# Attention and expert kernel: logits from 64-row f32 products of queries and keys, in place of split f32r products through a combined weight

## The reference, cut to what matters

```python
Q = (X @ Wq + bq).reshape(b, t, h, dq).transpose(0, 2, 1, 3)
K = (X @ Wk).reshape(b, t, h, dq).transpose(0, 2, 1, 3)
V = (X @ Wv).reshape(b, t, h, dq).transpose(0, 2, 1, 3)
R = (X @ Wr + br).reshape(b, t, h, nb).transpose(0, 2, 1, 3)
extra = jnp.einsum('bhtn,ntp->bhtp', R, D_ntT)
logits = jnp.einsum('bhtd,bhpd->bhtp', Q, K) / math.sqrt(dq) + bias + extra
W = jax.nn.softmax(logits, axis=-1)
A = jnp.einsum('bhtp,bhpd->bhtd', W, V)
return A.transpose(0, 2, 1, 3).reshape(b, t, h * dq) @ Wproj + bproj
```

## Time and profile before

| | |
|---|---|
| median of 3 runs | 1675.25 us (1672.22 to 1677.1) |
| profiled execution | 1675.05 us, its span 1673.3 us |
| PE busy | 1510.8 us, 90% |
| VectorE busy | 1066.7 us, 64% |
| ScalarE busy | 988.9 us, 59% |
| GpSimd busy | 804.1 us, 48% |
| mean granted TensorE clock | 0.958 |
| chain that ended last, by engine | PE 72%, DVE 9%, issue 8%, ACT 4% |

### The profile page before, as it was taken

The page is one execution under the profiler, slowest core; times in us unless marked ns, Lnnn a source line. Parts: engine busy times, 40 slices in busy tenths (PEclk is TensorE's granted clock), DMA queues, the critical chain, the costliest instruction groups (busy, mean ns, idle before and its releaser), DMA issues.

```text
span 1673.3 us, 42585 instructions
## 1 busy us (share of the span) xinstructions
PE 1510.8 (90%) x10864; PEld 1276.9 (76%) x10864; DVE 1066.7 (64%) x3749; ACT 988.9 (59%) x2999; POOL 804.1 (48%) x1515
## 2 busy tenths in 40 slices
PE   2555999999999999989999997998989898989997
PEld 2224887878878887878999996787878787877885
DVE  5585777777767777762211112787868786877775
ACT  2223776766766676755554443676757675766664
POOL 0322766666666666650000001665656565656654
PEclk8686999999999999999999998999999999999999
DMA  9774555655555555655666664565555555656552
GB/s 285 271 274 120 163 168 145 177 166 165 155 160 168 152 159 145 180 154 160 201 202 205 206 202 136 155 174 135 167 143 161 150 149 143 166 142 180 145 158 70
DMA packets 375709, 282.62 MB, mean 169 GB/s; under 512 B 16626, under 2 KB 349988, under 8 KB 375588
## 3 DMA queue, kind: packets, MB, share of 16 engines
q1 hardware_dynamic: 367396, 264.64, 53.9%
q0 software_dynamic: 8192, 16.79, 3.5%
HBM read 168.05 MB, written 113.26 MB: 168 GB/s over the span
## 4 chain that ended last, share of the span: by engine, by line
PE 72%; DVE 9%; issue 8%; ACT 4%; SPq 3%; DMA 2%; DVEq 1%; POOL 1%; ACTq 0%; POOLq 0%
PE ps L1336 11%; PE ps L1334 11%; PE ps L1335 11%; PE ps L1475 10%; PE ps L1433 10%; PE ps L1370 8%; PE ps L1487 6%; PE ps L1404 3%; ACT prob L826 2%; DVE logit L1137 2%; DVE gst L1088 1%; DVE probT L1111 1%; DVE acc L1176 1%; SPq L453 1%; PE ps L1352 1%
## 5 line engine op out<-in xcount | busy, mean ns | idle before, releaser
L826 ACT ACTIVATE prob<-logit,low 128x128 f32<-128x128 f32 (+1 forms) x1024 | 454.2, 446 | 149.4 <-DVE low L1137 123.3
L1111 DVE COPY probT<-ps 128x384 f32<-128x384 f32 x512 | 284.5, 556 | 204.5 <-PE ps L1433 192.6
L687 POOL TENSOR_SCALAR prob<-prob,inv 128x128 f32<-128x128 f32 x512 | 188.6, 368 | 346.3 <-DVE inv L1121 336.7
L1137 DVE CUSTOM_DVE_ANT_0 logit<-ps,extra 128x128 f32<-128x128 f32 (+1 forms) x1024 | 303.3, 353 | 0.7 <-PE ps L1336 0.4
L1433 PE MATMUL ps<-ident,prob 128*128 128x128 f32 x1536 | 264.0, 281 | 12.1 <-DVE probT L1111 7.3
L1475 PE MATMUL ps<-probT,val 128*64 128x256 f32 (+1 forms) x2048 | 203.1, 342 | 44.1 <-DVE probT L1111 42.7
L689 POOL TENSOR_SCALAR prob<-prob,inv 128x256 f32<-128x256 f32 x512 | 241.4, 472 | 0.0
L1475 PEld LDWEIGHTS ps<-probT,val 128*64 128x64 f32 x2048 | 131.8, 141 | 130.7 <-issue 82.6
L1433 PEld LDWEIGHTS ps<-ident,prob 128*128 128x128 f32 x1536 | 175.0, 142 | 48.2 <-issue 40.7
L1334 PE MATMUL ps<-key_hi,xq_hi 128*128 128x256 f32 (+1 forms) x512 | 194.9, 381 | 0.0
L826 ACT ACTIVATION_READ_ACCUMULATOR prob<-logit,low 128x1 f32 x1024 | 192.9, 188 | 0.0
(11 more groups left out here) (188 smaller groups left out, 3088.2 us busy)
## 6 DMA issues: line engine op xcount, KB each, us to landing
skew<-gst SPq DMA_DIRECT2D x256, 256.0 KB
extra<-skew SPq DMA_DIRECT2D x128, 512.0 KB, 3.9
extra<-skew SPq DMA_DIRECT2D x128, 256.0 KB, 3.6
w1b<-w_d SPq DMA_DIRECT2D x39, 514.0 KB, 3.5
w2b<-w_d SPq DMA_DIRECT2D x39, 320.0 KB, 3.3
x_place<-zero SPq DMA_DIRECT2D x39, 256.0 KB, 2.7
placed<-x_place SPq DMA_DIRECT2D x39, 256.0 KB, 3.7
y_place<-yrow SPq DMA_DIRECT2D x39, 256.0 KB, 2.2
```

What stands on the lines that cost most here:

```text
L687: nc.gpsimd.tensor_scalar(prob[:, h, 0:P], prob[:, h, 0:P], inv[:, h, 0:1], 1.0, ALU.mult, ALU.mult).then_inc(norm_made, 1)
L826: ins = nc.scalar.activation(prob[:, h % PB, a:b], logit[:, h % LB, a:b], ACT.Exp, scale=-1.0, bias=low[:, h % LB, t:t + 1], accum_out=tot ...
L1111: nc.vector.tensor_copy(probT[:, h % 4, :], ps[:, PT_BANK, 0:3 * P]).then_inc(pT_made, 1)
L1137: ins = nc.vector.tensor_tensor_reduce(out=logit[:, h % LB, a:b], in0=src, in1=extra[:, h, a:b], scale=1.0, scalar=BIG, op0=ALU.add, op1=A ...
```

## The change

- The combined weight is gone. `keys` now projects the queries (scaled) and the keys of a pair of heads, 128 output rows each, by six f32r products of 256 columns. ScalarE copies both as plain f32 (`qk`); the low part on VectorE is gone.
- `logits` is a plain f32 product of 64 rows per head. The two heads of a pair lie in the two halves of the rows and write two banks (`S_BANK`), which alternate by pair; VectorE waits for both blocks at once.
- The output products write the bank that the value products use (`HEAD_BANK`), per quad and without accumulation over quads. VectorE adds them to `acc` after each quad (`add_heads`), and the next value products wait for that.
- The order of a slot: keys, the first unit, logits, value or output products, even transposes, second unit, odd transposes. The odd head's transposes of a pair so come in the same slot as the even head's.
- The table of units: "v" and "r" stand in the first place, "g" in the second; all positions are copied by VectorE.
- In the preparation the transposes of Wq and Wk and their product go; Wq and Wk are corrected by column means (with bq as a broadcast) and split.

```diff
-        KEY_BANK, S1_BANK, S0_BANK, PT_BANK, HEAD_BANK, MISC_BANK, OUT_BANK = 0, (1, 2), 3, 4, 5, 6, 7
+        S_BANK, KEY_BANK, PT_BANK, HEAD_BANK, MISC_BANK = ((0, 1), (2, 3)), 4, 5, 6, 7
-        UNITS = [(0, 0, "g", 2, 1, 0), (1, 0, "r", 0, 0, 1), (1, 1, "g", 3, 0, 0), (2, 0, "g", 3, 1, 0),
...
+        UNITS = [(0, 0, "v", 0, 0, 0), (0, 1, "g", 3, 0, 0), (1, 0, "r", 0, 0, 1), (1, 1, "g", 3, 1, 0),
...
-            sp.dma_start(bq_r[:, :], bq.rearrange("(k d) -> k d", d=P)).then_inc(small_in, 16)
+            sp.dma_start(bq_bc[:, :], bq.partition_broadcast(P)).then_inc(small_in, 16)
...
# ScalarE
-                nc.scalar.copy(key_hi[:, pair % 2, :, :].rearrange("p n k -> p (n k)"),
-                               ps[:, KEY_BANK, :]).then_inc(key_high, 1)
+                nc.scalar.copy(qk[:, pair % 2, :, :].rearrange("p n k -> p (n k)"),
+                               ps[:, KEY_BANK, :]).then_inc(key_made, 1)
...
# VectorE, in a slot
-                    if here(i, j - 3, heads, start):
-                        copy_probs(i, 2 * (j - 3) + 1)
-                    if heads and (j + 1 < PAIRS or more):
-                        keys(i if j + 1 < PAIRS else i + 1, (j + 1) % PAIRS)
...
+                        wait_apart(dve, s_psum, i * PAIRS + j + 1, const_made)
+                        wait_apart(dve, prob_made, i * PAIRS + j + 1 - LB // 2, const_made)
...
+                    if j % 2 == 1 and here(i, j - 5, heads, start):
+                        add_heads(i, (j - 5) // 2)
                     if here(i, j - 2, heads, start):
...
                         copy_probs(i, 2 * (j - 2))
                     for n, kind, k, t, ahead in units_at(j, 1, more) if heads else []:
...
+                        positions(len(START) + i * len(UNITS) + n, i + ahead, k, t)
+                    if here(i, j - 2, heads, start):
+                        copy_probs(i, 2 * (j - 2) + 1)
...
+            def add_heads(i, quad):
+                dve.wait_ge(out_psum, i * QUADS + (quad + 1))
+                wait_from(dve, attn_added, i * QUADS + quad)
+                seq = i if quad >= 0 else i - 1
+                x = acc[:, at(2 * seq, 2), :]
+                nc.vector.tensor_tensor(x, ps[:, HEAD_BANK, 0:2 * E].rearrange("p (t e) -> p t e", t=2), x,
+                                        ALU.add).then_inc(attn_added, 1)
...
# TensorE
-                wait_from(pe, key_low, i * PAIRS + pair)
-                for n in range(2):
-                    h = 2 * pair + n
-                    mm = product(ps[:, KEY_BANK, n * T:n * T + T],
-                                 ((wm_hi[:, h, :], wm_lo[:, h, :]), (xq_hi[:, par, :], xq_lo[:, par, :])))
+                wait_from(pe, key_made, i * PAIRS + pair)
+                cols = slice(pair * P, (pair + 1) * P)
+                for w in range(2):
+                    mm = product(ps[:, KEY_BANK, w * T:(w + 1) * T],
+                                 ((wqk_hi[:, w, cols], wqk_lo[:, w, cols]), (xq_hi[:, par, :], xq_lo[:, par, :])))
...
-                product(ps[:, S0_BANK, 0:T].rearrange("p (n k) -> p n k", n=2),
-                        ((xq_hi[:, par, 0:P], xq_lo[:, par, 0:P]),
-                         (key_hi[:, pair % 2, :, 0:P], key_lo[:, pair % 2, :, 0:P]))).then_inc(s0_psum, 1)
...
-                product(ps[:, S1_BANK[pair % 2], :].rearrange("p (n k) -> p n k", n=2),
-                        ((xq_hi[:, par, P:T], xq_lo[:, par, P:T]),
-                         (key_hi[:, pair % 2, :, :], key_lo[:, pair % 2, :, :]))).then_inc(s1_psum, 1)
+                for q, k, cols in ((slice(0, P), slice(0, P), slice(0, P)), (slice(P, T), slice(0, T), slice(P, 3 * P))):
+                    for n in range(2):
+                        rows = slice(DQ * n, DQ * n + DQ)
+                        mm = nc.tensor.matmul(ps[:, S_BANK[pair % 2][n], cols], qk[rows, pair % 2, 0, q],
+                                              qk[rows, pair % 2, 1, k], start=True, stop=True)
+                mm.then_inc(s_psum, 1)
...
+                wait_from(pe, attn_added, i * QUADS + quad)
...
                     if heads and (j + 1 < PAIRS or more):
                         keys(i if j + 1 < PAIRS else i + 1, par if j + 1 < PAIRS else 1 - par, (j + 1) % PAIRS)
-                    if here(i, j - 3, heads, start):
-                        turn_probs(i, 2 * (j - 3) + 1)
                     if heads:
-                        logits(i, par, j)
                         units(i, par, j, 0, more)
+                        logits(i, j)
                     if j % 2 == 0 and here(i, j - 4, heads, start):
...
+                        values(i, (j - 4) // 2)
                     if j % 2 == 1 and here(i, j - 5, heads, start):
...
+                        outputs(i, (j - 5) // 2)
                     if here(i, j - 2, heads, start):
                         turn_probs(i, 2 * (j - 2))
                     if heads:
                         units(i, par, j, 1, more)
+                    if here(i, j - 2, heads, start):
+                        turn_probs(i, 2 * (j - 2) + 1)
```

More of the change, by code:

```diff
@@ L690, in sequence @@
                                                     ALU.mult, ALU.mult).then_inc(norm_made, 1)
-                    for n, kind, k, t, ahead in units_at(j - 1, 0, more) + units_at(j - 1, 1, more):
-                        if kind == "r" and heads:
+                    for n, kind, k, t, ahead in units_at(j, 0, more) if heads else []:
+                        if kind == "r":
                             round_weights(i + 1, k)
@@ L836, in sequence @@
                                        ps[:, HEAD_BANK, :]).then_inc(head_made, 1)
-                    for n, kind, k, t, ahead in units_at(j, 1, more) if heads else []:
-                        unit(len(START) + i * len(UNITS) + n, kind, k, t, i + ahead)
             def experts(b, u, k):
@@ L1168, in add_rows @@
                     wait_from(dve, fetched, (n + 1) * (PER * TOP * 16))
-                    dve.wait_ge(attn_added, done)
+                    dve.wait_ge(attn_added, QUADS * done)
                 else:
@@ L1207, in _ @@
                 for n, (kind, g, t) in enumerate(START):
-                    if kind == "g" and t == 0:
+                    if kind == "g":
                         positions(s0 * len(UNITS) + n, s0, g, t)
-                keys(s0, 0)
                 sequence(s0, s0)
@@ L1263, in _ @@
             nc.tensor.matmul(ps[0:NB, b, 0:WIN], bT[:, :], flip[:, :], start=True, stop=True).then_inc(prep_made, 1)
+            pe.wait_ge(attn_in, 80)
+            for w in range(2):
+                for k in range(2):
+                    nc.tensor.matmul(ps[:, QK_MEAN_BANK[2 * w + k], :], ones[:, :],
+                                     wqk_r[:, w, k * BANK:(k + 1) * BANK], start=True, stop=True).then_inc(mean_psum, 1)
+            pe.wait_ge(qk_centred, 2)
             for k in range(2):
@@ L1267, in _ @@
                                  start=True, stop=True).then_inc(mean_psum, 1)
+            pe.wait_ge(qk_centred, 5)
             nc.tensor.matmul(ps[:, WR_MEAN_BANK, 0:H * NB], ones[:, :], wr_r[:, :],
                              start=True, stop=True).then_inc(mean_psum, 1)
[L1271 to L1280 removed]
             pe.wait_ge(centred, 3)
@@ L1384, in _ @@
             pe.wait_ge(wr_split, 2)
+            pe.wait_ge(qk_low, 2)
             pe.wait_ge(basis_in, 3 * PER * 16)
@@ new lines, in values @@
+            def values(i, quad):
+                h = 4 * quad + 3
+                if quad == 0:
+                    pe.wait_ge(val_made, 4 * i + 2)
+                if quad == -2:
+                    pe.wait_ge(val_made, 4 * i)
+                pe.wait_ge(pT_made, i * H + h + 1)
+                wait_from(pe, attn_added, i * QUADS + quad)
+                for pair in range(2):
+                    for s in range(2):
+                        q = slice(pair * T, (pair + 1) * T) if s == 0 else slice(pair * T + P, (pair + 1) * T)
+                        p = slice(0, T) if s == 0 else slice(T, 3 * P)
+                        for n in range(2):
+                            hh = h - 3 + 2 * pair + n
+                            v = hh % H * DQ
+                            mm = nc.tensor.matmul(ps[DQ * n:DQ * n + DQ, HEAD_BANK, q],
+                                                  val[:, s, v:v + DQ], probT[:, hh % 4, p],
+                                                  start=(s == 0), stop=(s == 1), skip_group_check=True)
+                mm.then_inc(head_psum, 1)
@@ new lines, in outputs @@
+            def outputs(i, quad):
+                pe.wait_ge(head_made, i * QUADS + (quad + 1))
+                for t in range(2):
+                    for pair in range(2):
+                        mm = nc.tensor.matmul(ps[:, HEAD_BANK, t * E:(t + 1) * E],
+                                              headT[:, pair, t * P:(t + 1) * P],
+                                              wproj[:, (2 * quad + pair) % PAIRS, :],
```

(2 more changed lines are left out.)

205 lines of the change are left out of this document (57 added, 148 removed), and 6 rows, old and new, of the table UNITS.

## The result

The change makes the kernel slower: 1773.66 us (1773.27 to 1774.28) against 1675.99 in the same session, ratio 1.0587 [1.0569, 1.0606]. Forecast were 1763 us and a range of 1705 to 1835. The profiled execution's span is 1771.7 us, 98.4 more than before.

What follows compares the result with a forecast made beforehand. The prediction took TensorE to bound the kernel, busy 1510.8 of 1673.3 us. Slots +114, stalls -18, clock -9 and preparation +1 sum to +88 on 1675.05 us: 1763 us, range 1705 to 1835.

Steps and rivals of the forecast that it cites:

- main claim: In every slot, odd transposes wait for VectorE's copy of the even ones, making the kernel slower: 1763 us.
- Step 4: Order of transposes: round trip over VectorE's copy takes 1.29 us, so PE idles 0.67 us in every slot.
- Step 5: VectorE before the copy: its add delays odd slots; slots of 5.41 and 4.94 us, sequence 40.0, +114 us.
- Step 2: Queries and keys by pair: again six f32r products, 0.72 us, as before.
- Step 1: Logits of a pair: overlapped passes 0.66 us plus 0.14 switch, 0.80 us against 1.06 before.
- Step 3: PE's work per slot: -0.26 us in even, -0.12 in odd slots; 49 us gained if PE stayed the bound.
- Step 6: VectorE's loop jump: stall remains but slack hides 1.5 to 1.6 us of each of 12, -18; clock -9.
- Step 7: Preparation: products and transposes go, corrections and splits come, +1 us; start and drain of each half unchanged.
- A: Rival at PE's odd transposes: PE passes them while they wait and runs the next slot's keys; 1626 us, 6%.
- B: Rival on the logits: row halves do not overlap, +0.66 us in all 256 slots; 1932 us, 7%.
- C: Rival on the logits: row halves entered at no cost, 0.14 less in 256 slots; 1727 us, 20%.
- D: Rival on PE's clock: every sequence loses 1.7 us to a lower clock, +54; 1817 us, 9%.

Runs made afterwards that it cites:

- odd_next: The changed kernel with the odd head's transposes and their copy moved back to the next slot, behind the keys: 1673.38 us, ratio 0.9994.
- before_same_slot: The kernel before with the odd head's transposes and their copy moved to the end of the same slot: 1785.40 us, ratio 1.0653.
- add_late: The changed kernel with VectorE's add of the output products moved behind the even head's copy: 1755.21 us, ratio 1.048.
- one_half: The changed kernel with both heads' logits computed from rows 0 to 63: 1958.46 us, ratio 1.1696.
- logits_twice: `old_order` with the eight passes of each pair's logits issued twice in one block: 1828.14 us, ratio 1.0913.
- old_order: The change's projections, logits and banks, with the order, unit table and shared position copies of the kernel before: 1656.68 us, ratio 0.9904.

## Why the prediction was right, and where its terms were off

The main claim holds by its own steps. **Step 4**: the round trip from the even to the odd transposes is 1.37 us in both slots shown and in the median of all (1.29 forecast), PE idles 0.59 and 0.65 in it (0.67 forecast), and two runs with opposite edits (`odd_next` -100 us, `before_same_slot` +111) put the whole slowdown there. **Step 5**: reductions 1.12 (1.10), add 0.33 (0.36), copy to transposes 0.70 (0.70); `add_late` shows that the add holds PE. **Step 2** holds: transposes and keys take 1.07 us together (372.23 to 373.30), as forecast (0.35 + 0.72).

**Step 1, mis-sized.** The six passes cost 0.65, overlapped, as forecast (`one_half`, `logits_twice`). The switch was put at 0.14. It costs 0.09 of gap on entry (last product 373.77 + 0.235, next start 374.09), 0.20 within the block up to the next start, and the output products behind it take 0.99 us (374.95 to 375.94) instead of 0.89: 0.39 for entry and exit, about 0.2 each. The reading of the earlier trace rows had the fault already. It found 0.13 us too much within the block of value products and took 0.05 of it into the price of a switch. The single starts show the rest as the exit: the block's last couple holds PE for 0.21 us instead of 0.11 (1264.60 to 1264.81), and the first transpose behind it for 0.16. **Step 3** falls with it: in odd slots PE gains nothing (0.66 + 0.39 = 1.05 against 1.06) instead of 0.12, in even slots 0.20 (0.09 + 0.86 against 1.06 + 0.09) instead of 0.26. That is 0.8 us per sequence and 26 in all, not 49, and in the order of before, where logits adjoin no value products, nothing: `old_order` has 36.0 us. It is why `odd_next` missed its 1610 by so much. The other 1.8 us of its 37.2 over 35.4 is, within 0.2, the wait for the units' bank (some 1.6).

The slots: the odd one takes 5.08 us (372.23 to 377.31), forecast 4.94; the even one 5.54 (377.31 to 382.85), forecast 5.41. In the odd slot the 0.14 is the logits (0.95 against 0.80), in the even one the logits (0.95 against 0.89) and the round trip (0.08). The medians over the loops are much the same (5.07 to 5.11, and 5.45 to 5.55). Eight slots make a plain sequence 1.0 to 1.1 longer, 41.0 and 41.1 against 40.0, and those of before were a little shorter than I had read (36.1 and 36.6 in the mean). So the 32 sequences should have had 152 us in the sum, not 114.

**Step 6, too small.** It had VectorE's stalls unchanged. They are 32.7 us in twelve, at most 3.0, where they were some 42 us and reached 4.6. The one of 359.23:

```profile
358.10 1.52 PE L1412 MATMUL ps<-probT,val 128*64 128x256 f32 x16
359.23 0.18 DVE L1083 RECIPROCAL inv<-total 128x4 f32<-128x4 f32 x1 [2.98 <-issue]
...
361.60 0.52 PE L1381 MATMUL ps<-ident,prob 128*128 128x128 f32 x3 [1.27 <-DVE probT L1073]
```

PE waits for 1.27 instead of 0.59 us: 0.7 is all that is seen of the jump. Forecast was 0.6 in the first half, right, and 2.7 in the second, where the sequences with a jump are likewise only 0.6 longer than the plain ones. The clock had cost more before than I took, too. Two jump sequences of before, one of each half:

```profile
483.40:523.50 40.10, 37.52 (x274) 31.51 (x274) 27.70 (x104) 25.97 (x87) 24.27 (x47) 0.96 0.52 149
1226.21:1269.70 43.49, 38.84 (x274) 32.79 (x274) 29.67 (x114) 26.19 (x87) 24.19 (x47) 0.92 0.51 139
```

Of the twelve, three in the first half and five in the second have a granted clock of 0.96 or 0.92. Priced as in step 6 (the lost share times the length) that is 17 us where I took 9 to come back, and all of it does: after the change all twelve show 1.00. In all, a jump sequence was 2.9 and 5.6 us longer than a plain one before and is 0.5 and 0.6 longer after, which gives back 45 us where I had put down 27: 17 of clock instead of 9, and 28 of stalls shortened or hidden instead of 18.

**Step 7, the ends.** The preparation got 1.6 us longer (forecast 1). The first and last sequence of each half are among the 32, with 19 of the 152 us; with their drain they got only 9.4 longer. The whole is 152 - 45 + 2 - 10 = 99 us, against 98.4 measured. So the errors are +38 in the slots, -18 at the jumps and -10 at the ends. They have opposite signs, and that the total came within 11 us of the forecast is in part luck.

The rivals: A (PE passes the waiting transposes) did not happen, PE idles before them 224 times for VectorE's copy; B is excluded by `one_half`; C (a free switch) by `logits_twice`; D (the clock) went the other way (mean granted clock 0.972 after, 0.958 before).

## What to carry to other kernels

Where one PSUM bank goes from engine to engine and back, the work that stands between its two uses is part of its price: here 0.72 us of keys hid most of a round trip of 1.3 us, and moving the second transposes ahead of them cost 100 us in 256 slots, with no engine busier than before. Before an operation is made cheaper on TensorE, ask what its neighbours are: a tiled product between untiled ones pays its switch twice (0.39 us here, against 0.40 saved), beside another tiled one less. And take the arithmetic and the order of a change apart in two runs; here the arithmetic and the banks in the old order were 1% faster, the whole change 6% slower. And where a block is short, read its single starts: the exit from a tiled block is a gap that a row summing it up hides.

## What the hardware showed that I had not expected

- Leaving the row halves costs as much as entering. On either side a gap of 0.09 to 0.10 us (before 374.09, and before 374.95) is followed by a first pass that takes 0.10 longer than the others. The Trainium skill (TensorEngine Tiling, Key Properties) states that changing the tiling mode drains TensorE. The two gaps agree; the slow first pass behind the switch is a second part that the rule does not speak of.
- VectorE's stall at the jump is no constant. In the second half it was 4.1 to 4.6 us before, and at most 3.3 in the change and in every other run. `before_same_slot`, the old arithmetic in another order, has 2.8 to 3.3, so the new arithmetic is not needed for it. The Trainium skill (Runtime: NRT & Kernel Launch, Instruction fetch mechanics) states that a taken branch out of the fetched window forces a fetch of its target. A stall once per jump, with nothing to wait for, agrees; what makes it shorter stays open.
- PE's busy time can hide a wait: in `odd_next` it is 37.0 of 37.2 us, while its weight loads wait 35.3 us for VectorE over the whole run.
